# Attention results turned by TensorE transposes and copied by ScalarE instead of turned by VectorE and spread by DMA

## The reference

```python
def _L0_attn_ref(x, Wq, bq, Wk, bk, Wv, bv, gamma):
    ...
    scores = jnp.einsum('bmhd,bnhd->bhmn', q, k) / math.sqrt(dqk)
    scores = jnp.where(scores >= 0, scores, 0.2 * scores)
    beta = jax.nn.softmax(scores, axis=-1)
    out = jnp.einsum('bhmn,bnhd->bmhd', beta, v).reshape(B, M, C)
    return gamma * out + x
...
xn = _layernorm(x, axis=-1)
x = x + _L0_attn_ref(xn, ...) + _L0_ffn_ref(xn, ...)
```

## Time and profile before

| | us |
|---|---|
| median of 3 runs | 944.16 (942.27 to 945.29) |
| span of the profiled execution | 940.0 |
| PE, DVE, ACT, POOL busy | 861.2, 735.3, 691.3, 601.5 |
| attention, 12 and 20 passes | about 130 to 365 and 543 to 935 |

### The profile page before, as it was taken

The page is one execution under the profiler, slowest core; times in us unless marked ns, Lnnn a source line. Parts: engine busy times, 40 slices in busy tenths (PEclk is TensorE's granted clock), DMA queues, the critical chain, the costliest instruction groups (busy, mean ns, idle before and its releaser), DMA issues. The chain is left out here.

```text
span 940.0 us, 20061 instructions
## 1 busy us (share of the span) xinstructions
PE 861.2 (92%) x7499; PEld 348.9 (37%) x7500; DVE 735.3 (78%) x859; ACT 691.3 (74%) x811; POOL 601.5 (64%) x610
## 2 busy tenths in 40 slices
PE   0688269999999999999999999999999999999997
PEld 0444112222222224776867732222222222222222
DVE  5788889999999994101011099999999999999996
ACT  0578888888888887444453568888888888888886
POOL 3355247777777663999999226657567575765782
PEclk9999659999999999999999999999999999999999
DMA  7833101111111112233242210102112111210202
GB/s 214 303 66 74 32 27 33 51 40 51 47 27 36 25 38 88 90 121 116 93 138 71 94 44 22 40 19 59 36 25 59 25 36 29 70 29 13 69 18 55
DMA packets 71225, 59.36 MB, mean 63 GB/s; under 512 B 33770, under 2 KB 58178, under 8 KB 71136
## 3 DMA queue, kind: packets, MB, share of 16 engines
q1 hardware_dynamic: 61520, 48.06, 17.6%
q0 software_dynamic: 8192, 9.37, 3.6%
q10 hardware_dynamic: 1424, 0.76, 0.3%
HBM read 31.58 MB, written 30.02 MB: 66 GB/s over the span
## 5 line engine op out<-in xcount | busy, mean ns | idle before, releaser
L1133 DVE TENSOR_SCALAR ps<-ps 128x1024 f32<-128x1024 f32 x512 | 600.1, 1224 | 14.6 <-PE ps L825 11.7
L718 ACT ACTIVATE pr<-ps 128x1024 f32<-128x1024 f32 x512 | 523.4, 1023 | 104.5 <-PE ps L835 72.9
L855 PE MATMUL ps<-pr,vp 128*32 128x256 f32 x4096 | 327.2, 392 | 0.1
L835 PE MATMUL ps<-q,kz 64*128 64x512 bf16 x1024 | 200.7, 389 | 10.2 <-DVE ps L1133 4.4
L825 PE MATMUL ps<-q,kz 62*128 62x512 bf16 x1024 | 200.3, 389 | 2.9 <-DMA q<-parts_dram 1.3
L505 POOL DMA_INDIRECT xs<-eout,idxs x128 | 129.0, 1008 | 105.0 <-ACT pr L718 75.5
L490 POOL DMA_INDIRECT disp<-xn,idx x128 | 125.9, 984 | 50.8 <-issue 29.2
L835 PEld LDWEIGHTS ps<-q,kz 64*128 64x128 bf16 x1024 | 49.0, 93 | 225.7 <-DVE ps L1133 188.4
L1152 DVE TENSOR_TENSOR pr<-ps,parts 128x1024 f32<-128x1024 f32 x12 | 14.7, 1225 | 149.6 <-PE ps L920 149.6
L855 PEld LDWEIGHTS ps<-pr,vp 128*32 128x32 f32 x4096 | 81.1, 108 | 119.4 <-issue 117.6
L744 ACT ACTIVATE pr<-ps,b1s 128x512 f32<-128x512 f32 x96 | 65.8, 687 | 53.7 <-PE ps L909 53.7
(11 more groups left out here) (122 smaller groups left out, 530.3 us busy)
## 6 DMA issues: line engine op xcount, KB each, us to landing
moved<-att SPq DMA_DIRECT2D x480, 8.0 KB
disp<-pr SPq DMA_DIRECT2D x12, 512.0 KB, 4.9
eout<-pr SPq DMA_DIRECT2D x12, 512.0 KB, 2.9
y<-in_x SPq DMA_DIRECT2D x8, 512.0 KB, 8.1
out<-y SPq DMA_DIRECT2D x7, 512.0 KB
w<-in_w1t SPq DMA_DIRECT2D x12, 256.0 KB, 3.2
w<-in_w2t SPq DMA_DIRECT2D x12, 256.0 KB, 3.4
xs<-disp SPq DMA_DIRECT2D x6, 512.0 KB, 4.9
```

Source lines behind the costliest of these rows:

```text
L718: act.activation(pr[:, c % BUFS, 2 * pair:2 * pair + 2, :], ring[i % RING], ACT.Exp, scale=SLOPE).then_inc(S["exps"], 1)
L835: last = pe.matmul(ring[i % RING][:, k, :], kz[r:r + TILE, hg, pair, kc * P:(kc + 1) * P], q2[r:r + TILE, hg, qh * HALF:(qh + 1) * HALF], ...
L855: last = pe.matmul(acc[p % 2][32 * g:32 * g + 32, cols], vp[:, hg, kc, g, :], pr[:, c % BUFS, g % PAIRS * 2 + g // PAIRS, cols], start=(kc ...
L1133: dve.tensor_scalar(s, s, 0.0, 1.0 / SLOPE - 1.0, ALU.max, ALU.mult).then_inc(S["relu"], 1)
```

## The change

All passes now take one way. While pass `p + 1` runs, ACT copies `acc[p % 2]` to `ot` after the exponentials of unit 3 (`COPIED`); PE transposes one 128x128 piece in each of units 5, 6, 7 and 8 (`TURNED` and on), between `shifted` and `scores`, back into `acc[p % 2]`; ACT copies the turned bank to a new SBUF tile `res` after the exponentials of unit 9 (`RETURNED`); DVE takes the reciprocals ahead of the rectify of unit 11 (`INVERTED`); POOL multiplies `res` into `moved` and adds it to `y` straight away. The DVE block transpose, the 480 DMAs of `spread` and the tile `att` are gone. The last pass of each stretch is as it was.

```diff
-TURN = 5
+COPIED, TURNED, RETURNED, INVERTED = 3, 5, 9, 11
...
-            def spread(p):
-
-                sp.wait_ge(S["att_rdy"], quotients(p))
-                wait_done(sp, "y_att", p - 1)
-                for g in range(HG):
-                    for r in range(NR):
-                        sp.dma_start(moved[BLOCK * r:BLOCK * r + BLOCK, p % 2, g, :, :],
-                                     att[BLOCK * g:BLOCK * g + BLOCK, p % 2, r, :, :]).then_inc(S[f"spread{p % 2}"], 16)
...
             def quotient(p):
-
+                nonlocal scaled_results
                 pool.wait_ge(S["rg_rdy"], p + 1)
-                if p > 1:
-                    wait_done(pool, f"spread{p % 2}", 16 * HG * NR * spreads(p - 2))
...
+                wait_done(pool, "y_att", p - 1)
+                rows = res[:, p % 2, :].rearrange("p (t g c) -> p g t c", g=HG, c=BLOCK)[:, :, :, 0:DV]
+                inv_rows = rg[:, p % 2, :].rearrange("p (g t) -> p g t", g=HG).unsqueeze(3)
+                pool.tensor_tensor(moved[:, p % 2, :, :, :], rows, inv_rows.broadcast_to([P, HG, GT, DV]), ALU.mult
+                                   ).then_inc(S["att_rdy"], 1)
...
-                        if p > first + 1:
-                            settle(p - 2)
                         if p > first:
-                            quotient(p - 1)
+                            settle(p - 1)
...
             def evacuate(p):
 
                 act.wait_ge(S["pv"], TB * (p + 1))
-                act.wait_ge(S["att_rdy"], quotients(p - 2))
+                wait_done(act, "o_rdy", p - 1)
                 act.copy(ot[:, p % 2, :], acc[p % 2]).then_inc(S["acc_evac"], 1)
+
+            def take_back(p):
+
+                act.wait_ge(S["o_rdy"], p + 1)
+                wait_done(act, "y_att", p - 1)
+                act.copy(res[:, p % 2, :], acc[p % 2]).then_inc(S["turned"], 1)
...
                     exponentials(i)
+                    if i % UP == COPIED and i > first + UP:
+                        evacuate(i // UP - 1)
+                    if i % UP == RETURNED and i > first + UP:
+                        take_back(i // UP - 1)
...
-            def turn(p):
-
-                pe.wait_ge(S["acc_evac"], 1 + LAST.index(p))
-                for t in range(GT):
-                    last = pe.transpose(acc[p % 2][:, t * P:(t + 1) * P], ot[:, p % 2, t * P:(t + 1) * P], ident)
-                last.then_inc(S["o_rdy"], 1)
+            def turn(p, t):
+
+                if t == 0:
+                    pe.wait_ge(S["acc_evac"], p + 1)
+                last = pe.transpose(acc[p % 2][:, t * P:(t + 1) * P], ot[:, p % 2, t * P:(t + 1) * P], ident)
+                if t == GT - 1:
+                    last.then_inc(S["o_rdy"], 1)
...
                     shifted(i)
+                    if 0 <= i % UP - TURNED < GT and i > first + UP:
+                        turn(i // UP - 1, i % UP - TURNED)
                     if i + AHEAD < end and i != BH * NUB:
                         scores(i + AHEAD)
...
-            def turn(p):
-
-                dve.wait_ge(S["pv"], TB * (p + 1))
-                if p > 1:
-                    dve.wait_ge(S["att_rdy"], quotients(p - 2))
-                dve.transpose(ot[:, p % 2, :], acc[p % 2]).then_inc(S["turned"], 1)
-
             def denominators(p):
 
                 dve.wait_ge(S["turned"], p + 1)
-                rows = ot[:, p % 2, :].rearrange("p (q c) -> p q c", c=BLOCK)
-                dve.reciprocal(rg[:, p % 2, :], rows[:, :, DV]).then_inc(S["rg_rdy"], 1)
+                rows = res[:, p % 2, :].rearrange("p (t g c) -> p g t c", g=HG, c=BLOCK)
+                dve.reciprocal(rg[:, p % 2, :].rearrange("p (g t) -> p g t", g=HG), rows[:, :, :, DV]
+                               ).then_inc(S["rg_rdy"], 1)
...
-                    if i % UP == TURN and i > first + UP:
-                        turn(i // UP - 1)
-                    if i % UP == TURN + 1 and i > first + UP:
+                    if i % UP == INVERTED and i > first + UP:
                         denominators(i // UP - 1)
                     rectify(i)
```

More of the change, by code:

```diff
@@ L60 @@
 GB = 2
-TURN = 5
+COPIED, TURNED, RETURNED, INVERTED = 3, 5, 9, 11
 BLOCK = 32
-NR = P // BLOCK
 C_ID, C_TRI, C_KDIR, C_PDIR, C_RDIR, C_BO = 0, 128, 256, 384, 512, 640
@@ L154, in build @@
         rg = sb("rg", [P, 2, HALF // BLOCK])
-        att = sb("att", [P, 2, NR, GT, DV])
+        res = sb("res", [P, 2, HALF])
         moved = sb("moved", [P, 2, HG, GT, DV])
@@ L202, in build @@
                  "qz_init weighted at_rdy sum_rdy inv_rdy row_step route ones_rdy max_rdy off_rdy reset_rdy r_exp cnt_rdy pos_rdy ztile init_rdy kz_init "
-                 "ld0 ld1 vp_rdy s1 relu s2 exps pv acc_evac o_rdy turned rg_rdy att_rdy spread0 spread1 y_att "
+                 "ld0 ld1 vp_rdy s1 relu s2 exps pv acc_evac o_rdy turned rg_rdy att_rdy y_att "
                  "scat staged pool_step carry "
@@ L244, in build @@
         LAST = (BH * NPB - 1, B * NPB - 1)
[L246 to L252, removed]
         def pass_at(b, hg, qh):
@@ L346, in _ @@
                 operands_in(p)
-                if 0 < p < BH * NPB - 1:
-                    spread(p - 1)
             sp.wait_ge(S["scat"], 16 * GS)
@@ L364, in _ @@
             load_expert(0, 0)
-            spread(BH * NPB - 2)
             sp.wait_ge(S["pv"], BH * NPB * TB)
@@ L378, in _ @@
                 operands_in(p)
-                if p > BH * NPB:
-                    spread(p - 1)
                 if p % NPB == 0 and p > BH * NPB:
@@ L430, in _ @@
             added, combined = 0, 0
+            scaled_results = 0
             def quotient(p):
+                nonlocal scaled_results
                 pool.wait_ge(S["rg_rdy"], p + 1)
-                if p > 1:
-                    wait_done(pool, f"spread{p % 2}", 16 * HG * NR * spreads(p - 2))
[L437 to L440, removed]
+                wait_done(pool, "y_att", p - 1)
[3 more added lines that the diff above has]
+                                   ).then_inc(S["att_rdy"], 1)
+                scaled_results += 1
+                pool.wait_ge(S["att_rdy"], scaled_results)
+                pool.sem_inc(S["carry"], 1)
             def add_attention(p):
@@ L447, in add_attention @@
                 else:
-                    pool.wait_ge(S[f"spread{p % 2}"], 16 * HG * NR * spreads(p))
-                    pool.sem_inc(S["carry"], 1)
+                    quotient(p)
                 ys = y[:, bass.ds(b * TB + qh * GT, GT), hg * HG * DV:(hg + 1) * HG * DV].rearrange(
@@ L557, in results @@
                             value_rows(b + 1, 0)
-                        if p > first + 1:
-                            settle(p - 2)
                         if p > first:
-                            quotient(p - 1)
+                            settle(p - 1)
                     move(p, results)
-                settle(last - 1)
                 settle(last)
@@ L907, in expert @@
                     if n == 2 and first:
-                        turn(BH * NPB - 1)
+                        for t in range(GT):
+                            turn(BH * NPB - 1, t)
                     pe.matmul(ps[:, 2 + n % 4, :], w1[:, 2 * u * FFN + f * P:2 * u * FFN + (f + 1) * P],
@@ L937, in _ @@
             attention(BH, B)
-            turn(B * NPB - 1)
+            for t in range(GT):
+                turn(B * NPB - 1, t)
         @block.vector
@@ L1102, in _ @@
             last.then_inc(S["at_rdy"], 1)
-            def turn(p):
-                dve.wait_ge(S["pv"], TB * (p + 1))
-                if p > 1:
-                    dve.wait_ge(S["att_rdy"], quotients(p - 2))
-                dve.transpose(ot[:, p % 2, :], acc[p % 2]).then_inc(S["turned"], 1)
             def denominators(p):
                 dve.wait_ge(S["turned"], p + 1)
-                rows = ot[:, p % 2, :].rearrange("p (q c) -> p q c", c=BLOCK)
-                dve.reciprocal(rg[:, p % 2, :], rows[:, :, DV]).then_inc(S["rg_rdy"], 1)
+                rows = res[:, p % 2, :].rearrange("p (t g c) -> p g t c", g=HG, c=BLOCK)
+                dve.reciprocal(rg[:, p % 2, :].rearrange("p (g t) -> p g t", g=HG), rows[:, :, :, DV]
+                               ).then_inc(S["rg_rdy"], 1)
             def finish(p):
-                dve.wait_ge(S["o_rdy"], 1 + LAST.index(p))
+                dve.wait_ge(S["o_rdy"], p + 1)
+                dve.wait_ge(S["y_att"], p - 1)
                 rows = acc[p % 2].rearrange("p (t g c) -> p g t c", g=HG, c=BLOCK)
@@ L1123, in finish @@
                 dve.wait_ge(S["rg_rdy"], p + 1)
-                dve.wait_ge(S["y_att"], p - 1)
                 dve.tensor_tensor(moved[:, p % 2, :, :, :], rows[:, :, :, 0:DV],
```

## The result

The changed kernel takes 1,000.43 us (median of 4 runs, 997.06 to 1,001.83) against 943.72 us (4 runs, 942.27 to 945.29) for the kernel before: ratio 1.0609, 95% interval 1.0579 to 1.0638. It was forecast slower, at 973 us in a range of 950 to 984. Slower is right; the size isn't. The span of its profiled execution is 998.4 us.

A forecast was written before the change was run, and what follows sets the result against it. A loop through PE and ACT over two units was taken as the bound: 19.20 + 1.05 (transposes) + 0.14 (copies) = 20.39 us a pass against 19.43, x 30 = +28.8 us, giving 973 us, range 950 to 984.

The forecast's parts named there:

- The bound: In the attention passes a loop through PE and ACT over two units sets the pace, not DVE: 2.40 us a pair.
- The loop's 19.20 us a pass: 16 units of a pass through PE and ACT take 8 x 2.40 = 19.20 us, against 19.43 in the trace.
- DVE's transpose, 0.23 us a pass: Taking the block transpose off DVE gives back 0.23 us a pass; the rest hides in DVE's lead over PE.
- The transposes on PE, +1.05 us: Four lone transposes in units 5 to 8 cost 0.33 us each; units take 1.46 instead of 1.20 us, +1.05 a pass.
- Their price read off at 540 us: Gaps between half-array pairs and full-array matmuls at 540 us in the trace: 0.31 us into a transpose, 0.20 out of it.
- rival 2: Transposes on PE cost what they do in a row, 0.11 us each: 951 us, slower still; chance 0.16.
- The copies, +0.14 us: Of ACT's two copies a pass, the first is covered by a transpose; the second, behind unit 9, adds 0.14 us.
- The waits added: New waits come free in time; the reciprocal ahead of unit 11 takes 0.15 us of DVE, hidden by its lead: nothing.
- Rival 3: ACT's copies or the result chain through POOL bring more waits, one unit in each pass: some 1,009 us; chance 0.03.
- POOL's later results: POOL waits until unit 11 for the reciprocals, with paced DMAs queued behind, and makes up for it next pass: nothing.

The follow-up runs named there:

- with unit 13: The changed kernel with the reciprocals ahead of the rectify of unit 13 instead of 11: 971.61 us, ratio 1.0311 to the kernel before.

## Why the prediction was right and wrong

- **The bound: right.** DVE, at 99.6% busy, wasn't the bound. Cutting DVE's turning into two pieces, 4.8 us dearer in all, made the kernel 0.3% faster, and four transposes a pass on PE that nobody reads made it 3.4% slower. The loop's 19.20 us a pass was nearly reached (19.26). That ACT is in the loop rests on the two copies: they cost 0.20 us a pass beside its idle time. No run made a step of the loop shorter.
- **DVE's transpose, 0.23 us a pass: in line** with the 0.17 that the halves gave back.
- **The transposes on PE, +1.05 us: right.** 0.34 for one alone against 0.33, 1.47 a unit against 1.46, +1.09 a pass measured by itself. Their price read off at 540 us, from other matmuls of the same shapes, held; rival 2 with 0.11 each falls. Grouped in one unit the same four cost +0.52. The Trainium skill's rule that changing the tiling mode drains the engine (TensorEngine Tiling (Array Packing), section Tiling Modes) is in line with that: the price goes with the number of changes, not of transposes. No run here tells a drain from another cost of the change.
- **The copies, +0.14 us: about right** with unit 13: the pass of 20.46 less the loop's 19.20 and the transposes' 1.09 leaves 0.17. By themselves two uncovered copies cost 0.20, less than 0.28.
- **The waits added: this step failed.** It said that the reciprocal ahead of unit 11 takes 0.15 us of DVE, hidden by DVE's lead, and put the added waits at nothing. I went through the waits of PE, ACT and POOL and left out DVE's own, for ACT's second copy. The runs showed a wait of 1.19 us in each pass with the rectify of unit 11 behind it, which lengthens the pass by 0.88 us: 30 x 0.88 = 26 us of the 27 us by which the forecast was short. One or two units later it is gone. Rival 3 had a wait of about a unit in each pass and 1,009 us, but looked for it at ACT and POOL, and I gave it 0.03.
- **POOL's later results: right**, nothing was seen of them: with unit 13, later still, the time is what the loop gives.

What would have shown it ahead of time were the rows I used. In the earlier trace rows the exponentials of the `shifted` of 701.06 end at 702.51, 1.45 us after it starts, and a copy behind them adds 0.48: the copy behind unit 9 ends 1.93 us after `shifted` of unit 9 starts. DVE is done with the rectify of unit 9 before that `shifted` starts and needs 1.20 us for unit 10, so it comes to unit 11 after 1.20 us at the latest, 0.7 us or more before the copy ends. In the changed kernel it came there after 0.78 us (747.53 to 748.31), and the copy ended after 1.94. "After unit 9 on ACT" is in time behind "ahead of unit 11 on DVE".

## What to carry to other kernels

In a pipeline that several engines share, a unit's number is no time. Where work is handed from one engine to another, work out how many units the one runs ahead of the other, and put the waiting instruction behind that distance and a margin: one unit too early cost 28 us here, two 98 (some 38 of them by the lower clock), and one or two units more of distance cost nothing. Look for the bound as a loop of waits whose steps repeat, not as the busiest engine, and price an insertion by its neighbours: here a matmul of another tile shape cost the two changes around it, and putting four such matmuls together halved their price.

## What the hardware showed unexpectedly

A stall of 2.22 us on PE was followed by a lower granted clock (0.57 in the mean over 3.4 us, 0.939 over the whole execution against 0.979 in the changed kernel), a stall of 0.93 us wasn't. So a wait one unit longer cost 69 us, where the longer stall by itself makes 33: the slow steps behind it cost as much again. The same stall with the clock kept up was not tried, so this division rests on the steps in the timeline alone.
